# One order of work at the end of a block of experts, and two mask products a pair instead of three in windowed attention

## What is computed

```python
xq = mxfp8_qdq(routed)
h13 = jax.lax.ragged_dot(xq, jnp.swapaxes(w13q, 1, 2), counts)
h1, h3 = (h13[:, :hidden], h13[:, hidden:])
h = jax.nn.silu(h1) * h3
hq = mxfp8_qdq(h)
routed_out = jax.lax.ragged_dot(hq, jnp.swapaxes(w2q, 1, 2), counts)
shared = jax.nn.silu(xf @ sw1.T) * (xf @ sw3.T) @ sw2.T
return (shared + routed_sum).reshape(bs, slen, dim)
```

```python
mask = (q_idx >= k_idx) & (q_idx - k_idx <= WINDOW - 1)
scores = jnp.where(mask[None, None], scores, -jnp.inf)
probs = jax.nn.softmax(scores, axis=-1)
out = jnp.einsum('bhqk,bhkd->bhqd', probs, v)
return out @ w_o.T
```

## Time and profile before

| | us |
|---|---|
| median of 3 runs | 1379.28 |
| lowest and highest | 1376.93, 1383.08 |
| profiled execution | 1369.57 |
| its span (first to last instruction) | 1367.6 |
| TensorE busy in it | 1191.7 (87%) |
| VectorE busy in it | 871.5 (64%) |
| ScalarE busy in it | 612.1 (45%) |
| mean granted TensorE clock | 0.934 of full speed |

### The profile page before, as it was taken

How to read it: one execution, slowest core, us unless ns; L and a number is a source line. 1 busy time by engine, 2 the same in 40 slices (tenths; PEclk the granted TensorE clock), 3 DMA queues, 4 the chain that set the end, 5 groups by cost and what they waited for, 6 DMA issues and landing times.

```text
span 1367.6 us, 22966 instructions
## 1 busy us (share of the span) xinstructions
PE 1191.7 (87%) x7487; PEld 758.4 (55%) x7487; DVE 871.5 (64%) x2165; ACT 612.1 (45%) x1526; POOL 425.1 (31%) x569
## 2 busy tenths in 40 slices
PE   7688998899977959979999999999999950799995
PEld 3554664566853427646668436663366750465654
DVE  1687887754289896566754877658766453355552
ACT  1246777688182110247720117751277322466650
POOL 2162774654100001335530004430044327132232
PEclk9899999999978988999997999999999985799998
DMA  8064997000001000110021000000220342233214
GB/s 305 8 215 140 324 322 250 17 1 1 1 32 45 1 0 1 77 63 2 2 88 44 1 0 1 1 1 1 101 116 1 123 170 107 75 94 87 83 51 161
DMA packets 61171, 106.51 MB, mean 78 GB/s; under 512 B 5312, under 2 KB 49856, under 8 KB 57792
## 3 DMA queue, kind: packets, MB, share of 16 engines
q1 hardware_dynamic: 57216, 94.29, 20.5%
q0 software_dynamic: 3840, 10.75, 2.2%
HBM read 57.44 MB, written 47.59 MB: 77 GB/s over the span
## 4 chain that ended last, share of the span: by engine, by line
PE 70%; DVE 16%; POOL 6%; issue 4%; DMA 1%; ACT 1%; SPq 0%; POOLq 0%; DVEq 0%; ACTq 0%
PE ps L710 8%; PE ps L699 7%; PE ps L988 6%; PE ps L719 4%; PE ps L691 4%; PE ps L692 3%; PE ps L1042 3%; PE ps L1037 3%; PE ps L969 2%; PE ps L821 2%; POOL mem L1882 2%; PE ps L659 2%; PE ps L1060 2%; PE ps L893 2%; PE ps L873 1%
## 5 line engine op out<-in xcount | busy, mean ns | idle before, releaser
L1882 POOL TENSOR_SCALAR mem<-mem 128x512 f32<-128x512 f32 x256 | 177.7, 698 | 385.0 <-DVE mem L1199 381.8
L1194 DVE TENSOR_REDUCE mem<-ps 128x1 f32<-128x512 f32 x256 | 175.3, 687 | 108.2 <-PE ps L692 99.7
L1693 ACT ACTIVATE mem<-ps,mem 128x512 f32<-128x512 f32 x256 | 177.0, 695 | 12.6 <-DVE mem L1194 11.9
L699 PE MATMUL ps<-mem 128*128 128x128 f32 x1024 | 160.2, 280 | 12.8 <-POOL mem L1882 11.8
L1686 ACT ACTIVATE mem<-ps 128x512 f32<-128x512 f32 x192 | 115.9, 605 | 92.5 <-PE ps L699 92.1
L699 PEld LDWEIGHTS ps<-mem 128*128 128x128 f32 x1024 | 119.2, 142 | 68.2 <-POOL mem L1882 49.3
L691 PE MATMUL ps<-rounded_at 128*128 128x512 f32 x256 | 125.0, 488 | 11.5 <-DVE rounded_at L1183 10.4
L710 PE MATMUL ps<-mem 128*64 128x256 f32 x1024 | 124.9, 386 | 2.4 <-ACT mem L1686 2.4
L1661 ACT ACTIVATE rounded_at<-ps 64x512 fp32r<-64x512 f32 x64 | 37.8, 591 | 164.4 <-PE ps L971 153.2
L692 PE MATMUL ps<-rounded_at 128*128 128x512 f32 x256 | 103.2, 403 | 0.0
L1857 POOL TENSOR_SCALAR mem<-mem 128x1 f32<-128x1 f32 x48 | 9.1, 190 | 270.4 <-DVE mem L1134 250.9
(11 more groups left out here) (273 smaller groups left out, 2672.7 us busy)
## 6 DMA issues: line engine op xcount, KB each, us to landing
slots<-mem SPq DMA_DIRECT2D x15, 2312.0 KB, 9.8
mem<-in_f_w_dram SPq DMA_DIRECT2D x16, 1024.0 KB, 8.9
mem<-slots SPq DMA_DIRECT2D x96, 68.0 KB, 2.2
mem<-in_f_w_dram SPq DMA_DIRECT2D x24, 256.0 KB, 3.3
mem<-in_x_wq_dram SPq DMA_DIRECT2D x2, 2048.0 KB, 13.2
mem<-in_x_wo_dram SPq DMA_DIRECT2D x2, 2048.0 KB, 8.4
mem<-parts SPq DMA_DIRECT2D x16, 256.0 KB, 5.5
mem<-in_x_wqr_dram SPq DMA_DIRECT2D x1, 1536.0 KB, 6.5
```

The costliest lines, as they stand in the source:

```text
L699: mm = pe.transpose(ps[3 + j % 2][:, k * P:(k + 1) * P], PR[j % 6][:, k * P:(k + 1) * P], ident)
L1194: dve.tensor_reduce(nmax[:, i % 8:i % 8 + 1], ps[SB[lay][i % len(SB[lay])]][:, :], AX.X, ALU.max, negate=True)\
L1693: act.activation(PR[i % 6], ps[SB[lay][i % len(SB[lay])]][:, :], ACT.Exp, bias=nmax[:, i % 8:i % 8 + 1], accum_out=esum[:, i % 8:i % 8 + 1 ...
L1882: pool.tensor_scalar(PR[i % 6], PR[i % 6], rinv[:, i % 8:i % 8 + 1], 1.0, ALU.mult, ALU.mult)\
```

## The change

It has three parts.

1. VectorE, end of the first experts: the products w = 14 and 15 and the masked copies of set 1 are moved ahead of rounding 6; roundings 6 and 7 follow each other.
2. TensorE, there: the transposes of the hidden sets 2 and 3 are moved from ahead of all outputs to places behind output 0 and behind output 2. The outputs of this block use four banks, `ps[t % 4]`, in place of two, so that outputs 0 to 3 need no addition of VectorE before them; each of them waits for the L1347 product that frees its bank (`f_hh`). The transposes of X trail four tiles behind in place of two. Other blocks keep two banks.
3. Window attention: `KEEP` is 0 in place of 1. Pairs 3 to 23 have two mask products in place of three.

```diff
-        KEEP_FIRST, KEEP = 6, 1
+        KEEP_FIRST, KEEP = 6, 0
...
+        def output_bank(n, t):
+            return ps[t % 4 if n == 2 else 2 + t % 2]
...
+                behind = 4 if n == 2 else 2
                 for t in range(NT):
                     g = NT * n + t
-                    if g >= 2:
+                    if n == 2 and t in (1, 3):
+                        hidden_transposes(t // 2 + 2)
+                    if n == 2 and t >= 4:
+                        pe.wait_ge(y_added, g - 3)
+                    elif n != 2 and g >= 2:
                         pe.wait_ge(y_added, g - 1)
-                    product(t, ps[2 + t % 2][:, 0:D]).then_inc(o_ready, 1)
-                    if t >= 2 and not last:
-                        transposes(t - 2)
+                    product(t, output_bank(n, t)[:, 0:D]).then_inc(o_ready, 1)
+                    if t >= behind and not last:
+                        transposes(t - behind)
...
-                    if s >= 1:
+                    if s in (1, 2):
                         hidden_transposes(s - 1)
-                hidden_transposes(3)
...
             def experts_layer0_out(t, bank):
+                if t < 4:
+                    pe.wait_ge(f_hh, 13 + t)
                 pe.wait_ge(f_hm, 2 * (t // 4) + 2)
...
-                for w in range(16):
-                    k = NW8 + 8 + w // 2
+                def activated(w):
                     dve.wait_ge(f_hs, w + 1)
-                    dve.tensor_tensor(rawa[k % 2][:, (w % 2) * D:(w % 2 + 1) * D], ps[w % 4][:, D:2 * D], sh0[w % 4],
+                    dve.tensor_tensor(rawa[w // 2 % 2][:, (w % 2) * D:(w % 2 + 1) * D], ps[w % 4][:, D:2 * D], sh0[w % 4],
                                       ALU.mult).then_inc(f_hh, 1)
-                    if w % 2 == 1:
-                        dve.wait_ge(f_hh, w + 1)
-                        quantised(k, rawa[k % 2], piece(w // 2))
-                    if w in (4, 8):
-                        masked(w // 4 + 1)
-                    if w == 10:
-                        hidden_masked(0)
-                    if w == 14:
+
+                for n in range(8):
+                    if n < 7:
+                        activated(2 * n)
+                        if n in (2, 4):
+                            masked(n // 2 + 1)
+                        if n == 5:
+                            hidden_masked(0)
+                        activated(2 * n + 1)
+                    if n == 6:
+                        activated(14)
+                        activated(15)
                         hidden_masked(1)
+                    dve.wait_ge(f_hh, 2 * n + 2)
+                    quantised(NW8 + 8 + n, rawa[n % 2], piece(n))
```

More of the change, by code:

```diff
@@ L500, in output_and_layernorm @@
                 if not last:
-                    for t in range(NT - 2, NT + 1):
+                    for t in range(NT - behind, NT + 1):
                         if t < NT:
@@ L778, in experts_layer0 @@
                     mm.then_inc(f_up, 1)
-                def hidden_transposes(s):
-                    pe.wait_ge(q_d, NW8 + 8 + 2 * s + 2)
-                    if s == 0:
-                        pe.wait_ge(f_qt_ev, 4)
-                    if s >= 2:
-                        pe.wait_ge(f_ht_ev, s - 1)
-                    dst = ps[6 + s % 2][:, :].bitcast(BF16).rearrange("p (c t) -> p c t", c=DC)
-                    for t in range(4):
-                        for c in range(2):
-                            mm = pe.transpose(dst[:, c, t * P:(t + 1) * P], q8[:, s, t, c * P:(c + 1) * P], identb)
-                    mm.then_inc(f_ht, 1)
                 for s in range(4):
@@ L807, in experts_layer0, with hidden_transposes @@
                         mm.then_inc(f_h, 1)
-                    if s >= 1:
+                    if s in (1, 2):
                         hidden_transposes(s - 1)
-                hidden_transposes(3)
+            def hidden_transposes(s):
+                pe.wait_ge(q_d, NW8 + 8 + 2 * s + 2)
+                if s == 0:
+                    pe.wait_ge(f_qt_ev, 4)
+                if s >= 2:
+                    pe.wait_ge(f_ht_ev, s - 1)
+                dst = ps[6 + s % 2][:, :].bitcast(BF16).rearrange("p (c t) -> p c t", c=DC)
+                for t in range(4):
+                    for c in range(2):
+                        mm = pe.transpose(dst[:, c, t * P:(t + 1) * P], q8[:, s, t, c * P:(c + 1) * P], identb)
+                mm.then_inc(f_ht, 1)
             def experts_layer0_out(t, bank):
+                if t < 4:
+                    pe.wait_ge(f_hh, 13 + t)
                 pe.wait_ge(f_hm, 2 * (t // 4) + 2)
@@ L1130, in output_and_layernorm @@
                     dve.wait_ge(o_ready, g + 1)
-                    dve.tensor_tensor(X[:, t, :], ps[2 + t % 2][:, 0:D], X[:, t, :], ALU.add).then_inc(y_added, 1)
+                    dve.tensor_tensor(X[:, t, :], output_bank(n, t)[:, 0:D], X[:, t, :], ALU.add).then_inc(y_added, 1)
                     dve.wait_ge(y_added, g + 1)
```

## The result

| | us |
|---|---|
| before, median of 11 runs (lowest, highest) | 1377.39 (1373.60, 1383.08) |
| after, median of 11 runs (lowest, highest) | 1363.6 (1360.41, 1372.41) |
| ratio, 95% interval | 0.9909, 0.9892 to 0.9926 |
| profiled execution of before, its span | 1369.57, 1367.6 |
| profiled execution of after, its span | 1361.36, 1359.4 |

The medians differ by 13.8 us. The ratio, which is taken over all runs, makes it 12.5 us, with an interval of 10.2 to 14.9, and the forecast was 11.5. The time itself was forecast as 1367.8 and is 1363.6. Of the 4.2 between them 1.9 are the kernel before, whose median went from 1379.28 over three runs to 1377.39 over eleven, and 2.3 are the larger difference. The two profiled executions differ by only 8.2.

What follows compares the result with a forecast made beforehand. TensorE was taken to bound the kernel, with VectorE setting the time up to 515.9 at the experts' end. Gains of 6.5 (experts) and 5.0 (mask products), together 11.5 off 1379.28, gave 1367.8; range 1362.0 to 1373.0.

Steps and rivals of the forecast that it cites:

- Output 0: End of the first experts: TensorE's first output can start at 505.95, 10.9 us earlier, needing only sets 0 and 1.
- The low clock on output 0: First experts' outputs: TensorE's clock falls during the wait, so output 0 loses 2.6 us, between 1.7 and 3.4.
- VectorE's wait for set 3: First experts' outputs: VectorE, ready at 521.2, waits 2.6 us for the copy of set 3's transposes, the new late step.
- Output 4: First experts' outputs: output 4 starts at 529.7 in place of 537.04, a gain of 7.3 us.
- The second fall of the clock: TensorE's idle 2.7 us before output 4 may lower the clock again; costs 0 to 1.7, taken as 0.8.
- The tail: Behind 558.76: a denser tail could keep the clock high and give up to 1.7 us back; nothing counted.
- The mask products: Window attention: 21 products gone, pair 3 gives nothing, the other 20 give 0.25 each, 5.0 us; ends 3.5 and 5.2.
- The margin of GpSimd: Window attention: GpSimd is next behind TensorE; its margin shrinks by 0.25 to 0.1 us, more in the longer pairs.
- A: Rival: the clock holds and the overlap is full, over outputs and window attention; gain 15.2, time 1364.1; chance 0.14.
- B: Rival: GpSimd or VectorE takes TensorE's place in window attention; gain 8.0, time 1371.3; chance 0.12.
- C: Rival: the first experts' outputs move but gain nothing, only the mask products' gain is left; 1374.3; chance 0.04.
- D: Rival: the clock falls within window attention without the repeated mask product; slower, about 1402; chance 0.06.

Runs made afterwards that it cites:

- set 3 earlier: Changed kernel with the transposes of hidden set 3 behind output 1 in place of output 2; median 1351.90, ratio to the kernel before 0.9860.
- after again: The changed kernel, unchanged, run and profiled a second time; median 1356.94 against 1370.77 of the kernel before, ratio 0.9896.
- five products: Changed kernel with KEEP = 3, five mask products a pair in place of two; 1377.78, one run.
- experts alone: Changed kernel with KEEP = 1, the third mask product back, so only the two parts at the end of the first experts; 1368.64, ratio 0.9937.
- TensorE's order alone: Changed kernel with VectorE's loop of the kernel before and the third mask product back; 1373.3, one run.
- no mask product: Changed kernel without any mask product in pairs 3 to 23, that part of the computation left out; 1353.38, one run.
- masks alone: Kernel before with KEEP = 0 and nothing else; 1371.42 against 1377.56, ratio 0.9949.
- clock held: Changed kernel with 34 unused products ahead of output 0 and 10 ahead of output 4 filling TensorE's waits; 1354.34, ratio to the kernel before 0.9877.
- clean pair: Second profiles of the unchanged kernel before and the changed kernel, both without VectorE's long routing wait; 200.56 and 189.58 ahead of it, 10.98 us apart.

## Why the prediction was right

**Output 0.** Forecast 10.9 earlier, measured 10.9 (22.68 to 11.79). The sum of VectorE's rows (1.4 for four products, 5.4 for the copies) held to 0.1, since moving instructions on one engine doesn't change what each takes.

**The low clock on output 0.** The loss of 2.6 was taken from 7.49 for transposes and output in the earlier trace rows. It measured 1.8 in after (6.67 less 4.88) and 2.0 to 2.4 in the other six profiles with this order. The direction was right and the term too large by 0.2 to 0.8: the price of a fallen clock depends on how soon it comes back after work resumes, and that was 5.2 us in the earlier trace rows and 3.7 in after (0.66 over 504 to 508 puts it near 506.7, with output 0 from 503.06).

**VectorE's wait for set 3.** Forecast 2.6, measured 2.02, and 2.24 in the second profile. The mechanism was right, and it was the new late step: removing it (set 3 earlier) advanced output 4 by 2.3 and, with the clock that then held, the next stage by 4.0. The prediction named this wait and priced it, and it could have said that one output earlier would remove it.

**Output 4.** Forecast 7.3 earlier, measured 8.1. The 0.8 are those of output 0, passed on through set 3. In the second profiles it is 7.2 (42.17 to 35.00), as the kernel before itself came 0.7 sooner there.

**The second fall of the clock.** Counted at 0.8, between 0 and 1.7. It fell in the profile of after, in after again and with five products, each time for 1.7; it didn't with the experts alone, TensorE's order alone and no mask product, which have the same order on TensorE up to there and the same idle time. Experts alone, TensorE's outputs 3 and 4:

```profile
521.85 3.66 PE L830 MATMUL ps<-mem 128*128 128x256 bf16 x32
528.03 1.13 PE L826 MATMUL ps<-mem 128*128 128x256 f32 x4 [2.52 <-DVE mem L1140]
529.00 3.66 PE L830 MATMUL ps<-mem 128*128 128x256 bf16 x32
```

An idle time of 2.52 to 2.53 between full work on both sides went one way or the other from execution to execution. The six differ in one thing ahead of it: output 0 with its transposes took 6.67, 6.88 and 6.93 where the clock fell, and 7.09, 7.29 and 7.71 where it held. So the clock that came back later at output 0 was the one that held at output 4; six executions are few for a rule. For a forecast from the rows of before a value between the ends was the right way to count it. The Trainium skill, "TensorE: Matmul & The Clock Gate", section "Part 1: The HAM clock gate (the "warmup" mystery)", says that the monitor runs free of the kernel, so the place at which the level changes varies from run to run. The six executions with this gap agree: three at the low clock and three at the full one for the same output.

**The tail.** Up to 1.7 was left uncounted for projections that might keep their clock. They did in after, and gave the 1.7. This goes with the new order on TensorE: from the next stage to pair 0 it is 36.8 in eight of its ten profiles and 38.5 in two (experts alone, no mask product), where the old order has 38.1 to 38.5 in all four. So the term should have been counted for the most part. The first pairs took 1.8 of it back in after, but they came out short or long under both orders, so that the two cancel is luck. The forecast's upper end has 1.0 from the tail, for which no row is given.

**The mask products.** Forecast 5.0, measured 4.3 (135.19 to 130.89 with the masks alone). Pair 3 gave nothing, as said. The step that was mis-sized is the price of one, 0.25 from 0.75 for three and 1.90 for eight: a row of the timeline also holds the end of its last product, 0.1 to 0.2 that lies beside the next row. The difference of two rows of the same view with unlike counts leaves it out: 1.90 for eight less 0.82 for three is 1.08 for five more, 0.216 each, the price that the runs gave. The rows of before held it. The margin of GpSimd was sized too small, and with it the lower end of 3.5: two products a pair more could go for 0.6 us of waits in 19 pairs. The same is seen in after, where two products have a row of 0.60, and the row is shorter than before by 0.22.

**The rivals.** A (clock held, full overlap) didn't come by itself; as an experiment it brought the next stage 3.7 earlier than in after, and the median 2.6 lower; it takes VectorE's wait away as well, so it isn't a test of the clock alone. B (GpSimd takes over) is excluded down to no mask product at all, where it costs 0.6 over 19 pairs. C is excluded by output 4. D (the clock falls in window attention) is excluded by 1.00 in every stretch from pair 4 on, with two, three, five and no mask products.

**The sum.** 6.5 and 5.0 were forecast. Measured on the clean pair, 4.3 are the mask products and 6.7 the rest. The first term was 0.2 low and the second 0.7 high, and the total of 11.0 stands beside 11.5. That it came so near is in part luck: the low clock on output 0 and the mask products were counted too high, the new order's gain in the projections not at all. The ratio of the runs says 12.5, and 14.3 for after again; what is beyond 11.0 isn't explained, and lies within the intervals. One of the forecast's signs of being wrong, a stage elsewhere that loses what these gain, did come up in part: the first two spans differ by 8.2, little more than its 7, and only the second pair of profiles, without the wait, shows that the loss isn't the change's.

## What to carry to other kernels

When one engine waits for another through a chain of small steps, give it work that doesn't need the chain and reorder both engines together: one side alone gave nothing and 2.3 of 8.1 us here. Then look at once for the wait that the new order makes: the one priced in the prediction was worth 4.0 us more up to the next stage, 2.3 for the wait and 1.7 for the clock, for a move of one line. Price a removed instruction by the difference of two groups with unlike counts, not by a group's time over its count, and compare executions stage by stage from a common row, since code that wasn't changed moved by 5 to 7 us between two profiles.

## What the runs showed of the hardware

- VectorE can wait 13.9 to 14.6 us in front of an instruction whose products have long been made, in some sessions (each on its own chip) and not in others; it cost 7.0 of the span.
- The clock over an idle time of 2.5 us between full work fell in three executions and held in three, with the same order on TensorE. Each fall cost 1.7 on the output behind it. It fell where output 0 had taken 6.67 to 6.93, and held where it had taken 7.09 to 7.71.
- A product of 128x512 in bf16 behind its like costs 0.215 us at a clock of 1.00, by the three counts of 2, 3 and 5 products a pair.
- The clock stays at 1.00 in window attention even without any mask product, with TensorE busy for 10.00 of 10.00 us (630 to 640); with the small products of the earlier trace rows it is 0.51 at the same share. The share of busy time alone doesn't tell the level.
